# Window attention with per-head scores on 32 rows each: four PSUM banks, another order of TensorE, another sharing of the copies of the values

## What is computed

```python
# layer 0: x = x + conv_ref(group_norm(x)); 4 heads of 32 channels, windows of 7 x 7 = 49
x = jnp.roll(x, (-3, -3), axis=(1, 2))
q, k, v = jnp.split(x @ w_qkv, 3, axis=-1)                 # to windows: b, head, window, 49, 32
dots = jnp.einsum('bhwid,bhwjd->bhwij', q, k) * 32 ** -0.5
dots = dots + bias[None, None, None] + MASK[None, None]    # bias by relative position
attn = jax.nn.softmax(dots, axis=-1)
out = jnp.einsum('bhwij,bhwjd->bhwid', attn, v)            # back to b, h, w, 128
out = jnp.roll(out @ w_out + b_out, (3, 3), axis=(1, 2))
```

## Time and profile before

| | before |
|---|---|
| time, median of 3 runs | 1777.92 us (1776.94 to 1779.36) |
| profiled execution, its own time | 1780.86 us |
| its span | 1779.2 us |
| mean granted clock of TensorE | 0.996 |
| PE busy | 1738.9 us (98%) |
| DVE busy | 1511.7 us (85%) |
| ACT busy | 1227.8 us (69%) |
| POOL busy | 1080.4 us (61%) |

### The profile page before, as it was taken

How to read it: one execution, slowest core, us unless ns; L and a number is a source line. 1 busy time by engine, 2 the same in 40 slices (tenths; PEclk the granted TensorE clock), 3 DMA queues, 4 the chain that set the end, 5 groups by cost and what they waited for, 6 DMA issues and landing times.

```text
span 1779.2 us, 56159 instructions
## 1 busy us (share of the span) xinstructions
PE 1738.9 (98%) x18976; PEld 1575.7 (89%) x18976; DVE 1511.7 (85%) x4580; ACT 1227.8 (69%) x3219; POOL 1080.4 (61%) x1200
## 2 busy tenths in 40 slices
PE   7999999999999999989999999999999999979997
PEld 6888888888888888879999999999999999979997
DVE  7888888888888888778888888888888888848887
ACT  5887887888778887756666666666666666635554
POOL 6888888888888888843333333333333333448994
PEclk9999999999999999999999999999999999999999
DMA  5433433343343432314444444444453444457885
GB/s 168 111 106 98 109 104 107 101 111 106 102 107 102 110 106 66 83 46 68 72 68 68 72 68 69 68 68 68 78 94 68 70 68 76 68 121 275 307 307 193
DMA packets 361502, 189.38 MB, mean 106 GB/s; under 512 B 220176, under 2 KB 348672, under 8 KB 356864
## 3 DMA queue, kind: packets, MB, share of 16 engines
q1 hardware_dynamic: 360064, 184.61, 42.8%
q10 hardware_dynamic: 1152, 1.13, 0.2%
HBM read 107.80 MB, written 77.87 MB: 104 GB/s over the span
## 4 chain that ended last, share of the span: by engine, by line
PE 52%; issue 28%; POOL 17%; DVE 1%; DMA 1%; POOLq 0%; ACT 0%; ACTq 0%; SPq 0%; DVEq 0%
POOL la_rstd L1018 12%; PE k_psum L349 7%; PE k_psum L299 6%; PE k_psum L292 6%; PE k_psum L317 6%; PE k_psum L333 6%; PE k_psum L1478 5%; PE k_psum L365 5%; PE k_psum L1488 5%; PE k_psum L283 5%; POOL la_spread L1012 3%; POOL la_tn L1023 2%; DMA t<-la_tn 0%; POOLq L42 0%; DMA wa_group<-in_group 0%
## 5 line engine op out<-in xcount | busy, mean ns | idle before, releaser
L1012 POOL TENSOR_SCALAR la_spread<-la_mv 128x4 f32<-128x4 f32 (+1 forms) x203 | 45.8, 226 | 477.4 <-DVE la_mv L1123 477.3
L618 POOL TENSOR_TENSOR wa_prob<-wa_prob,wa_peak 128x784 f32<-128x784 f32 x128 | 194.8, 1522 | 116.9 <-DVE wa_peak L484 116.9
L959 ACT ACTIVATE la_ve<-k_psum 128x256 f32<-128x256 f32 x196 | 75.6, 386 | 232.9 <-PE k_psum L840 232.9
L1018 POOL TENSOR_TENSOR la_rstd<-la_spread,k_exponent 128x4 f32<-128x4 f32 (+1 forms) x203 | 207.5, 1022 | 17.2 <-POOL la_spread L1012 0.4
L828 PE MATMUL k_psum<-la_uT,la_wt 128*128 128x256 f32 x784 | 201.9, 380 | 0.0
L625 POOL TENSOR_TENSOR wa_prob<-wa_prob,wa_inv 128x784 f32<-128x784 f32 x128 | 194.8, 1522 | 11.4 <-DVE wa_inv L445 11.4
L1078 DVE SCALAR_TENSOR_TENSOR la_fqk<-k_psum,la_raised 128x512 f32<-128x512 f32 x196 | 135.2, 690 | 63.7 <-ACT la_raised L951 63.2
L476 DVE TENSOR_TENSOR wa_prob<-k_psum,wa_bias 128x784 f32<-128x784 f32 x128 | 124.9, 976 | 66.2 <-PE k_psum L317 66.1
L1560 ACT ACTIVATE sc_y<-k_psum,sc_cols 128x224 f32<-128x224 f32 x246 | 110.1, 448 | 89.3 <-PE k_psum L1488 89.3
L951 ACT ACTIVATE la_raised<-k_psum,la_minus_one 128x512 f32<-128x512 f32 x196 | 134.8, 688 | 45.6 <-PE k_psum L828 45.3
L525 ACT ACTIVATE wa_kb<-k_psum,wa_own 128x392 f32<-128x392 f32 x256 | 136.6, 584 | 36.2 <-PE k_psum L292 36.1
(11 more groups left out here) (137 smaller groups left out, 5146.1 us busy)
## 6 DMA issues: line engine op xcount, KB each, us to landing
t<-la_tn SPq DMA_DIRECT2D x392, 66.0 KB, 4.3
la_xc<-x SPq DMA_DIRECT2D x196, 128.0 KB, 3.4
wa_xT<-in_x_cm SPq DMA_DIRECT2D x124, 196.0 KB, 3.4
sc_tb<-t SPq DMA_DIRECT2D x16, 1386.0 KB, 8.5
out<-sc_ob SPq DMA_DIRECT2D x16, 1344.0 KB, 5.5
wa_xw<-in_x_tok SPq DMA_DIRECT2D x64, 224.0 KB, 2.7
wa_xw<-in_x_tok SPq DMA_DIRECT2D x64, 168.0 KB, 2.4
x<-wa_y SPq DMA_DIRECT2D x64, 168.0 KB, 2.9
```

Source lines behind the costliest of these rows:

```text
L618: nc.gpsimd.tensor_tensor(s, s, peak[:, k % S, :].unsqueeze(2).broadcast_to([128, PAIRS * HEADS, WIN]), ALU.subtract).then_inc(lowered, 1)
L1018: nc.gpsimd.tensor_tensor(rstd[:, n % S, used], spread[:, used], exponent[:, used], ALU.pow).then_inc(rooted, 1)
```

## The change

- `scores` makes one product for each window and each single head: 32 rows (the head's channels), 49 columns of weights, 49 moving columns. There are 32 products instead of 16, each head writes a bank of its own (banks 3 to 6, the first 196 columns). The masked second copy of the keys goes: `kb` becomes `kT`, `own` is dropped, and `keys_out` is one copy.
- The same four banks hold `b_ot` (banks 3 and 4, from column 196 on) and `b_y` (banks 5 and 6, from column 196 on). So the writers of a bank have to wait for the readers of its other part: `attend` and `project` wait for `biased` of the newest scores, and `scores` waits for `attended_out` of unit n-4 and `residual` of unit n-5.
- TensorE's order is new: `attend` of unit n-4 stands right behind `queries(n)`, `project` handles n-5. The pipeline has one step more (NU + 7), `JOIN` is one later, SP stores n-6, VectorE's residual handles n-5.
- `prob` is laid out as pair, head, window half; `add_bias` reads four banks and writes with another stride. The bias table exists once and not once for each slot.
- Of the four copies of the values ScalarE makes three, VectorE one.
- `attended_out` is four copies and not three. The residual of a three-tile unit is two instructions and not one.
- ScalarE's order: `keys_out`, `queries_out`, `attended_out`, and then as before.
- The linear attention's banks are numbered otherwise (`b_at` is the last), with releases to match.

The core of the diff:

```diff
-        b_q, b_k, b_v, _, _, b_pt, b_ot, b_y = bank
-        b_s = psum[:, 3 * 512:5 * 512].rearrange("p (a b) -> p a b", a=2)
+        b_q, b_k, b_v, _, _, _, _, b_pt = bank
+        b_heads = psum[:, 3 * 512:7 * 512].rearrange("p (a b) -> p a b", a=HEADS)
+        SCORED = PAIRS * WIN
+        b_s = b_heads[:, :, 0:SCORED]
+        b_ot = b_heads[:, 0:2, SCORED:SCORED + ROWTOK // 2]
+        b_y = b_heads[:, 2:4, SCORED:SCORED + 2 * C]
...
-        run = dict(first=-AHEAD, last=NU + 6, unroll=XS)
-        JOIN = NU - 3
+        run = dict(first=-AHEAD, last=NU + 7, unroll=XS)
+        JOIN = NU - 2
...
                     at_least(pe, biased, n)
+                    at_least(pe, o_out, n - 3)
+                    at_least(pe, summed, n - 4)
                     apart(pe, pe_passed)
                     for w in range(NWC):
...
-                        for hp in range(2):
-                            heads = slice(2 * HD * hp, 2 * HD * hp + 2 * HD)
-                            mm = nc.tensor.matmul(b_s[part, hp, w // 2 * 2 * WIN:(w // 2 + 1) * 2 * WIN],
-                                                  qT[heads, k % S, c:c + WIN], kb[heads, k % S, :, c:c + WIN], start=True, stop=True)
+                        for head in range(HEADS):
+                            rows_ = slice(HD * head, HD * (head + 1))
+                            mm = nc.tensor.matmul(b_s[part, head, w // 2 * WIN:(w // 2 + 1) * WIN],
+                                                  qT[rows_, k % S, tokens], kT[rows_, k % S, tokens], start=True, stop=True)
...
                     if h == 0:
                         pe.wait_ge(v_out, n + 1)
+                        pe.wait_ge(biased, min(n + 4, NU))
...
                     pe.wait_ge(o_out, n + 1)
+                    pe.wait_ge(biased, min(n + 5, NU))
...
                 def step(n, k, other):
                     queries(n, k)
+                    attend(n - 4, k - 4, 0)
+                    attend(n - 4, k - 4, 1)
                     turn_probabilities(n - 3, k - 3, 0)
-                    project(n - 4, k - 4)
+                    project(n - 5, k - 5)
                     values(n, k)
                     group_moments(n, k)
                     turn_probabilities(n - 3, k - 3, 1)
                     scores(n, k)
-                    attend(n - 3, k - 3, 0)
-                    attend(n - 3, k - 3, 1)
                     keys(n + 1, k + 1)
                     other()
...
-                    for par in range(2):
-                        src = b_v[par * WPAD:par * WPAD + WIN, :].rearrange("p (w a b c) -> p w a b c", w=PAIRS, a=2, b=2)[:, :, :, 1 - par, :]
-                        to = (1 - par) * WPAD
-                        last = nc.vector.tensor_copy(vb[to:to + WIN, k % S, :, par, :, 1 - par, :], src)
-                    last.then_inc(v_out, 1)
+                    src = b_v[0:WIN, :].rearrange("p (w a b c) -> p w a b c", w=PAIRS, a=2, b=2)[:, :, :, 1, :]
+                    nc.vector.tensor_copy(vb[WPAD:LANES, k % S, :, 0, :, 1, :], src).then_inc(v_out, 1)
...
-                    for slot in range(2):
-                        last = nc.scalar.activation(kb[:, k % S, slot, :], b_k[:, 0:ROWTOK], ACT.Identity, scale=own[:, slot:slot + 1])
-                    last.then_inc(k_out, 1)
+                    nc.scalar.activation(kT[:, k % S, :], b_k[:, 0:ROWTOK], ACT.Copy).then_inc(k_out, 1)
...
                 def step(n, k, other):
+                    keys_out(n, k)
+                    queries_out(n, k)
                     attended_out(n - 4, k - 4)
-                    keys_out(n, k)
                     probabilities_out(n - 3, k - 3, 0)
-                    queries_out(n, k)
                     values_out(n, k)
```

## The result

The changed kernel takes 1797.61 us (median of 4 runs, 1797.12 to 1799.27), the kernel before 1778.59 us in the same session (4 runs, 1776.94 to 1779.36): ratio 1.0112, 95% interval 1.0100 to 1.0125, 19.0 us slower. The profiled execution of after has a span of 1795.5 us, that of before 1779.2, so the traces differ by 16.3. The range held the time; the likeliest case, 1774.0, was wrong in sign.

A forecast was written before the change was run, and what follows sets the result against it. TensorE's matmuls, one behind the other, were taken to bound the window stage: -12.3 us from 123 full steps, +5.3 from aggregate waits, +3.0 at the seam, so -4.0 and 1774.0 us. Range 1761 to 1800.

The forecast's parts named there:

- the likeliest case: Whole kernel: 1774.0 us against 1777.92 before, a gain; 1766 to 1784, chance 0.46.
- What bounds the kernel: Window attention stage: TensorE's matmuls one behind the other set the step, 5.82 us in the mean.
- The scores: TensorE's scores in each step: eight turns of 0.052 plus 0.15 give 0.57 us, 0.25 less than now.
- the feeding of the queue: TensorE's queue at the scores: 4.8 ns an instruction, 128 of them, would make the scores 0.75 us.
- The pace of the starts: Tiles of the scores: eight start within 0.06 us; the skill's 4 ns rule gives 0.032, about 6 us lower in time.
- The order of TensorE: TensorE's new order in each step: changes of array shape cost 0.15 us more, bounds 0.05 and 0.25.
- Attend behind add_bias: Attend waits for add_bias of the step before: covered by 0.29 us; if uncovered, 0.1 to 0.3 a step.
- Steps with aggregate: Once in eight steps VectorE's aggregate delays the residual and the scores by 0.35 us; 15 times, +5.3 us.
- The copies: ScalarE and VectorE: one keys copy dropped, one values copy moved to ScalarE; effect on the time 0.
- The seam: Passage from window to linear attention: pipeline one step longer, linear attention joins later; +3 us, bounds 0 and +6.
- The sum: Whole kernel: -12.3 + 5.3 + 3.0 = -4.0 us on the profiled 1780.86, so 1774.0 against the median.
- rival 2: TensorE's queue is fed too slowly: scores 0.75 us, +0.08 a step in place of -0.10; 1796 us, chance 0.14.

The follow-up runs named there:

- the best version: Kernel before, with the first turn of the probabilities right behind attend only for units 8 to 119: 1774.59 us against 1777.18, ratio 0.9983.
- the version with the early turn everywhere: Kernel before, with the first turn of the probabilities right behind attend for all units: 1780.46 us against 1777.48, ratio 1.0019.

## Why the prediction was right or wrong

- **What bounds the kernel**: right. TensorE's matmuls one behind the other set the step in all kernels; VectorE and ScalarE got lighter and it brought nothing.
- **The scores**: the step that failed. Predicted 8 x 0.052 + 0.15 = 0.57, measured 0.77, which is 0.05 less than the 0.82 of before and not 0.25 less: 0.20 in each of 123 steps, 25 us. The pace of a turn was right for the first half: 32 started in 0.22, and the third and fourth eight came 0.046 behind the one ahead. What the sum left out is that the pace isn't kept: matmuls 33 to 64 take 0.41 more. The bound that the prediction had set aside, the feeding of the queue, comes nearest with 0.75. But its two parts, a rate of 4.8 ns an instruction and a stock that stands ready, are not what the traces show:
  - *The rate.* The 4.8 ns are counted from the start of a wait that itself lasts 0.05 us; from its end it is 4.0. In the run with half of the scores TensorE's sequencer passes the 64 instructions behind such a wait in 0.19 us (from 404.28 to the next wait at 404.46), 2.9 ns each. So a rate alone doesn't forbid the 3.3 that the 0.052 wanted.
  - *The stock.* In the steady steps the sequencer passes the last wait ahead of the scores 0.22 to 0.44 us before they start; where TensorE waits for the residual it does so only 0.06 before. And yet, of these 15 groups 13 take 0.76 us, no more than the 0.77 of the others, and again start their first 32 in 0.23 (the other two take 0.82 and 0.90). So what the head start could put ready is worth nothing:

```profile
428.83 0.83 PE L322 MATMUL k_psum<-wa_kT,wa_qT 32*49 32x49 f32 x64 [0.49 <-DVE wa_y L465]
429.59 0.60 PE L295 MATMUL k_psum<-wa_xn,wa_wqkv 128*128 128x392 f32 x1
```

  With or without a head start the sequencer is as a rule through with all 128 instructions 0.53 to 0.54 us after the first start, so 64 pass quickly and the other 64 wait for something. A reading that fits is that TensorE takes in some 64 instructions and an entry comes free only as its instruction ends: each lasts 0.2 us, and the first new start after the 32 comes 0.24 to 0.27 after the group's. In the steady steps of the run with half of the scores the sequencer gets past the 64 only 0.10 us or more after the first start, though it had 0.2 to 0.4 us before it, and the last transpose of the turn ends 0.07 after that start. That is argued from the traces and was not tested by itself, so what holds the second half back stays open; shown is that it is the place behind 32 others and not the matmuls.
- **The pace of the starts**: within an eight the starts are 7 ns apart (8 in 0.05 us), as the four of before were (4 in 0.02). The Trainium skill, "TensorE: Matmul & The Clock Gate", part 3, has some 4 ns for each further tile. No row here shows so little. Eights did follow each other at 0.046, but only in the first half, and the 6 us that the prediction worked out by this rule did not come. The same page, part 1, has starts no closer than some 25 ns. The 64 starts in 0.64 us are 10 ns each, and the measurement decides.
- **The order of TensorE**: right, +0.15 predicted, +0.147 measured, with the terms where they were put (queries +0.09, first turn +0.06). The run with the order alone gives 17.4 us (16.8 at the last scores of its trace), 123 x 0.147 = 18.1.
- **Attend behind add_bias**: right. The cover, 0.29 by the prediction, held in all steady steps; the wait shows once, at the last unit, where keys and queries no longer stand between them: 1.12 us ahead of the attend at 778.88.
- **Steps with aggregate**: the mechanism right, the size too small. The scores start 0.56 late, 0.49 of it idle, in place of 0.35, and in one step the wait is 2.8 us where before had a stall of 1.8 already; some 8.7 us in place of 5.3. Here is VectorE in such a step, the one whose scores start at 428.83:

```profile
425.80 0.37 DVE L420 BATCH_NORM_AGGREGATE wa_spread<-wa_stats 128x2 f32<-128x48 f32 x1
...
426.85 0.95 DVE L443 TENSOR_REDUCE wa_total<-wa_prob 128x16 f32<-128x784 f32 x1
...
427.84 0.25 DVE L449 RECIPROCAL wa_inv<-wa_total 128x16 f32<-128x16 f32 x1
428.01 0.36 DVE L463 TENSOR_TENSOR wa_y<-k_psum,wa_xb 112x256 f32<-112x256 f32 x1
428.29 0.28 DVE L465 TENSOR_TENSOR wa_y<-k_psum,wa_xb 112x128 f32<-112x128 f32 x1
```

  aggregate with its two followers took 1.05 us up to `add_up`, not 0.73 (L423 lasted 0.65, its line L419 in before 0.34 in the step of the earlier trace rows); why is open. Against that the split residual is shorter, 0.28 + 0.28 = 0.56 for 0.72. Both together make 0.32 - 0.16 = 0.16 more than predicted. And the scores start 0.25 after the residual's end (428.57 to 428.83), where the prediction had 0.11 for the release: 0.29 + 0.16 + 0.14 = 0.59, against 0.56 measured.
- **The copies**: their own time was rightly nothing; that the moved copy covers the residual, 0.17 us in each step with aggregate, was not said.
- **The seam**: +3 predicted, 0 measured. The extra step's work moved out of the others, and what waits it has lie beside the linear attention's.
- **The sum**: 123 x (0.15 - 0.05) + 8.7 + 0 = 21 against 20.9 at the last scores; 19.0 in the medians. With 0.75 for the scores, rival 2 gave 1796 for the measured 1797.6, at a chance of 0.14. Its number for the scores was nearly right and its reason only in part: it foresaw longer gaps towards the end of the 64, which came, but from a rate of 4.8 ns for all of them, where the first 64 instructions need 2.9 to 3.5 ns each and the others 6. That the two make nearly the same sum is luck. That the measured time lies within the range of 1761 to 1800 is no merit of the forecast's own case, which had a gain.

## What to carry to other kernels

When matmuls are cut into smaller tiles, count the instructions before the width of the array: here 64 instructions (32 float32 matmuls) went at full pace and every further one cost some 6 ns, so products cut to half their columns gained 0.05 us of the 0.25 that was forecast. Order TensorE's work so that tiles of one shape stand together; each added change of shape cost some 0.15 us, three times what the smaller scores saved. A bank that is shared by two results ties its next writer to the reader of the other part, so look at what is queued ahead of that reader in the rare steps as well.

## What the runs showed that was not expected

The granted clock behind a wait of TensorE. In the best version TensorE waits at the seam for 1.09 us ahead of a turn, as the kernel before does for 1.10, and yet only in the former does the clock fall. The stretch of 764 to 766 us, of before and then of the best version:

```profile
764.00:766.00 2.00, 1.86 (x15) 1.65 (x16) 2.00 (x5) 1.24 (x5) 1.55 (x3) 1.00 0.43 121
```

```profile
764.00:766.00 2.00, 2.00 (x23) 1.72 (x21) 1.72 (x5) 0.55 (x1) 1.93 (x2) 0.50 0.00 0
```

0.50 is the level of 1.2 GHz; it lasts about 3 us and costs 1.3 (the last scores start 1.95 us earlier than before, the linear attention's first product 0.62). The same happens elsewhere, and as little regularly. Behind a wait of 1.78 us at unit 22 the clock falls in the best version, at a cost of 1.7, and not in the version with the early turn everywhere. At the same place it falls behind waits of 2.2 us (aggregate later) and 2.9 (two copies each), and not behind the 2.8 of after. Why the same idle time brings it down in one execution and not in the other is open. Two things follow. A gain ahead of a stretch with idle time can be lost in part. And a difference of 1 to 3 us between two traces of this kernel should be held against the clock of the same stretch before another cause is named. The other surprise is above: the three long steps of the linear attention in before, 2.5 us in all, in a stage in which every instruction is the same.
